# A message pass over 200,000 edges: two subtractions move from VectorE to GpSimd between its gathers, the additions of products vary by step, and one transpose in four becomes a copy

## The chip, the cores and the metric

The kernel runs on one core of a Trainium2 chip. The metric is the device time of the whole program in microseconds, as the median of several runs. The engines are named as in the profile: PE (TensorE; PEld is its weight load), DVE (VectorE), ACT (ScalarE), POOL (GpSimd), and SP, which issues DMAs.

## The reference, cut to what matters

The program is a graph network of four layers over 12,500 nodes and 200,000 edges, each layer followed by a residual addition and a layer norm. The change is in the third layer alone:

```python
xs = concat([x[src, :8], x[dst, :8]])                       # 16 scalars an edge
xv = concat([x[src, 8:].reshape(E, 8, 3), x[dst, 8:].reshape(E, 8, 3)])
h = 2.0 ** 0.5 * relu(emb @ W1 / 10.0 ** 0.5)               # 16 hidden units an edge
w = (h @ W2 / 16.0 ** 0.5).reshape(E, 7, 16, 8)             # seven 16x8 matrices an edge
s_out = PW_S * (einsum('eu,euw->ew', xs, wa_s) + INV_SQRT3 * einsum('eui,ei,euw->ew', xv, y1, wb_s))
...                                                          # g_out and v_out in the same manner
edge_ftr = concat([TANH_GAIN * tanh(s_out), (TANH_GAIN * tanh(g_out))[:, :, None] * v_out]) * norm[:, None]
out = segment_sum(edge_ftr, dst, N)
```

The weights of an edge depend on the edge through its 16 hidden units h. So the sum is over the units: what PE computes per unit from the edge's node values is multiplied by h and added over the 16 units.

## The kernel before, in words

The third layer's edge work is the function `l2_pass` (L1759). The edges lie in 128 partitions, 1,568 tiles of 128 edges. They are worked through in 28 chunks of 56 tiles; a chunk is 14 steps q of 4 tiles, and a step is two pairs, so that a chunk has 28 pairs `pr`. Every engine has its own program, written out by hand for one chunk and looped over two chunks (buffers b = 0 and 1); the order on each engine is the order in that code, and semaphores tie the engines together.

In step q of chunk c the engines do this:

- PE (`one_chunk` at L2001) makes the products of the first pair of step q + 1, the transposes of step q + 2, half of the sums of step q - 1, the products of the second pair, and the other half of the sums. `products` (L1973) writes two tiles of PSUM per pair. `transposes` (L1964) turns per tile the node values `zs` (two transposes of 64 columns, beside each other in the array) and the hidden units `hs` (one of 64 columns at L1969 and one more of the first 32 of them at L1970, which lands in rows 64 to 95). `sums` (L1989) adds the products over the units with an identity matrix: one float32 matmul of 192 columns for each unit that is left, `KEPT` = 12 of 16.
- DVE (`one_chunk` at L2324) multiplies the products of a pair with h and with the vector values (`pair`, L2257: L2267 and L2270), and after each second pair adds the last `ADDED` = 4 of the 16 units onto the first 4 (`add_units`, L2276). Between pairs it has the work of the next chunk, whose place is a pair number: two scans that fill in the destination rows (`fill_scan`, pairs 4 and 5), the terms and sums of the edge's direction (`p_terms`, `p_sum`, pairs 7 to 11; the last sends `p_done`), `unit_rest` (pairs 13 and 18), and `leave` (pair 19). Of the chunk before it has the six steps of `message`, pairs 12 to 17.
- ACT (`one_chunk` at L2140) copies the transposed tiles from PSUM to SBUF (`turn`: L2053 and L2054), takes the sums out (`summed`, L2058), and at half steps j = 2q + half does copies for the next chunk and the chunk before.
- POOL gathers the source rows of each tile by an indirect DMA (`row_gather`, L204, called at L1960), 56 a chunk into `z[b]`. It may begin chunk c + 3 when ACT has taken chunk c + 1 out of that buffer, which is at j = 4 of chunk c.

The split of the hidden units: h is kept as three bfloat16 parts, high, middle and low, in `hs`. ACT casts the high part (`unit_part` step 0, j = 10, sends `h_high`). `unit_rest` step 0 subtracts it from h into `rest_h` (L2283, sends `h_left`); ACT casts the middle part (`unit_part` step 1, j = 15, sends `h_mid`); `unit_rest` step 1 subtracts that too (L2286, sends `h_least`); ACT casts the low part (`unit_part` step 2, j = 20). `rest_h` lies in the tile `spread`, where the direction terms lay before, so step 0 waits for `p_done` as well. The chunk's first transposes come at step 12 of the chunk before.

There are three buffers of products in PSUM and three in SBUF (`prod`). DVE's pair of a step waits until PE has summed the step that used its buffer; in the last step of an odd chunk that is the step two back, elsewhere three or four, or two at a chunk's second step (L1859 and L1862).

Of the kernel before, what the change touches and what calls it, by code (L numbers as in the profile page):

```python
# [20 lines left out]
BF16 = mybir.dt.bfloat16  # L21
# [3 lines left out]
ALU = mybir.AluOpType  # L25
# [3 lines left out]
P = 128  # L29
# [35 lines left out]
def gnn_kernel(nc, x, src, dst, emb_t, attr3, attr5, edge_w, edge_w1, l0_w, lam, cheb_w, cheb_b,  # L65
# [25 lines left out]
    with top:  # L91
# [1667 lines left out]
        def l2_pass():  # L1759
# [6 lines left out]
            n = T // CH // 2  # L1766
            NC = 2 * n
            COLS = NG * M
            ADDED = 4
            KEPT = 16 - ADDED  # L1770
            gathered = gather_signals("l2")
            with ExitStack() as st:
                def sb(name, shape, dt=F32):
# [26 lines left out]

                p_t = ps("p_t", [P, 7 * 512])
                p_z = ps("p_z", [P, 1024], F16)
                p_zt, p_ht = p_z[:, 0:4 * P], p_z[0:96, 4 * P:8 * P].bitcast(BF16)
                p_sum6 = p_t[:, 6 * 512:6 * 512 + 4 * COLS]

                def scalar_part(k, t):
# [16 lines left out]
                h_left = signal("h_left")  # L1823
                h_mid = signal("h_mid")
                h_least = signal("h_least")
                units_added = signal("units_added")
                starts_in = signal("starts_in")
                starts_taken = signal("starts_taken")
# [42 lines left out]
                with nc.Block() as block:  # L1871
# [80 lines left out]
                    @block.gpsimd  # L1952
                    def _(pool):
                        row_gather(pool, fill[:], table, first_row[:]).then_inc(s_agg, 16)
                        with pool.Fori(0, n) as i:
                            for b in range(2):
                                pool.wait_ge(idx_in[b], 16 * (i + 1))
                                pool.sem_inc(chunks_begun, 1)
                                for t in range(CH):
                                    row_gather(pool, z[b][:, t, :], table, idx[b][:, t:t + 1]).then_inc(gathered[b], 16)  # L1960

                    @block.tensor
                    def _(pe):
                        def transposes(b, q):  # L1964

                            for t in range(4):
                                for half in range(2):
                                    nc.tensor.transpose(p_zt[64 * half:64 * half + 64, t * P:(t + 1) * P], zs[b][:, 4 * q + t, :], ident_h[:])
                                nc.tensor.transpose(p_ht[0:64, t * P:(t + 1) * P], hs[b][:, 4 * q + t, :], ident_b[:])  # L1969
                                last = nc.tensor.transpose(p_ht[64:96, t * P:(t + 1) * P], hs[b][:, 4 * q + t, 0:32], ident_b[:])  # L1970
                            last.then_inc(transposed, 1)

                        def products(c, b, q, half, first=False):  # L1973
# [15 lines left out]
                        def sums(c, b, q, part, first=False):  # L1989

                            if part == 0:
                                pe.wait_ge(units_added, c * Q + q + 1)
                                if q >= 1 or not first:
                                    pe.wait_ge(red_out, c * Q + q)
                            for k in range(part * KEPT // 4, (part + 1) * KEPT // 4):
                                last = nc.tensor.matmul(p_sum6, ident[:], prod[prod_buffer(b, q)][:, :, k, :],  # L1996
                                                        start=(k == 0), stop=(k == KEPT - 1))
                            if part == 3:
                                last.then_inc(red_made, 1)

# [44 lines left out]
                    def _(act):  # L2045
                        A = nc.scalar

                        def turn(c, q, first=False):

                            act.wait_ge(transposed, c * Q + q + 1)  # L2050
                            if q >= 2 or not first:
                                act.wait_ge(t_made, c * PRS + 2 * q - 2)
                            A.activation(zt[q % 2], p_zt, ACT.Copy)  # L2053
                            A.activation(ht[q % 2], p_ht, ACT.Copy).then_inc(zt_ready, 1)  # L2054

                        def summed(c, b, q):
                            act.wait_ge(red_made, c * Q + q + 1)
# [82 lines left out]
                        def one_chunk(c, b, times, first=False, second=False, more=True):  # L2140
                            before = not first
                            nxt, other = c + 1, 1 - b
                            for q in range(Q):
                                for half in range(2):
                                    j = 2 * q + half
                                    if half == 0:
                                        if q >= 2:
                                            summed(c, b, q - 2)
                                        elif before:
                                            summed(c - 1, other, Q - 2 + q)  # L2150
                                    elif q + 2 < Q:
                                        turn(c, q + 2, first)
                                    elif more:
                                        turn(nxt, q + 2 - Q)
                                    if more:
                                        if j in (0, 1):
                                            fill_mask_half(nxt, j, first or second)
                                        if j in (2, 3):
                                            starts_half(nxt, j - 2)
                                        if j == 4:  # L2160
                                            take(nxt, other, times, first)
                                        if j in (6, 7):
                                            dst_half(nxt, other, j - 6)
                                        if j == 10:
                                            unit_part(nxt, other, times, 0)
                                        if j == 13:
                                            high(nxt, other)
                                        if j == 15:
                                            unit_part(nxt, other, times, 1)
                                        if j == 20:  # L2170
                                            unit_part(nxt, other, times, 2)
                                        if j == 21:
                                            low(nxt, other)
                                    if before:
                                        if j == 5:
                                            tanhs(c - 1, other)
                                        if j in (8, 9):
                                            msg_mask_half(c - 1, j - 8)
                                        if j in (18, 19):
                                            msg_half(c - 1, j - 18, second)  # L2180

                        for half in range(2):
                            fill_mask_half(0, half, first=True)
# [28 lines left out]
                    def _(v):  # L2212
# [59 lines left out]
                        def add_units(c, b, q):  # L2272

                            v.wait_ge(t_used, c * PRS + 2 * q + 2)
                            of = prod[prod_buffer(b, q)]
                            V.tensor_tensor(of[:, :, 0:ADDED, :], of[:, :, 0:ADDED, :], of[:, :, KEPT:16, :], ALU.add).then_inc(units_added, 1)  # L2276

                        def unit_rest(c, b, step):

                            if step == 0:  # L2280
                                v.wait_ge(p_done, c + 1)
                                v.wait_ge(h_high, c + 1)
                                V.tensor_tensor(rest_h, hid[b][:], hs[b][:, :, 0:16], ALU.subtract).then_inc(h_left, 1)  # L2283
                            else:
                                v.wait_ge(h_mid, c + 1)
                                V.tensor_tensor(rest_h, rest_h, hs[b][:, :, 16:32], ALU.subtract).then_inc(h_least, 1)  # L2286

                        def message(c, b, times, step, first=False):

# [34 lines left out]
                        def one_chunk(c, b, times, first=False, second=False, more=True):  # L2324
# [4 lines left out]
                            for pr in range(PRS):  # L2329
# [1 line left out]
                                if pr % 2 == 1:  # L2331
                                    add_units(c, b, pr // 2)
                                if more:
                                    if pr in (4, 5):
                                        fill_scan(nxt, pr - 4)
                                    if pr == 7:
                                        p_terms(nxt, other, 0, times)
                                    if pr == 9:
                                        p_terms(nxt, other, 1, times)
                                    if pr in (10, 11):  # L2340
                                        p_sum(nxt, pr - 10)
                                    if pr == 13:
                                        unit_rest(nxt, other, 0)
                                    if pr == 18:
                                        unit_rest(nxt, other, 1)
                                    if pr == 19:
                                        leave(nxt, other)
                                if not first and 12 <= pr < 18:
                                    message(c - 1, other, here - other, pr - 12, second)

                        V.memset(mask[:, :, 0], 0.0)
                        V.memset(tail[:], 0.0).then_inc(fill_done, 1)
# [5 lines left out]
                            p_terms(0, 0, e, 0)  # L2358
                        for step in range(2):
                            p_sum(0, step)  # L2360
                        for step in range(2):
                            unit_rest(0, 0, step)
                        leave(0, 0)
                        one_chunk(0, 0, 0, first=True)
                        one_chunk(1, 1, 1, second=True)
# [80 lines left out]
```

## Time and profile before

| | us |
|---|---|
| median of 3 runs (range) | 13048.11 (13040.12 to 13057.17) |
| the profiled execution | 13047.31 |
| its span in the profile | 13045.3 |
| busy in the span: PE / DVE / ACT / POOL | 5831.6 / 5177.0 / 1973.6 / 7561.5 |
| the pass of the change, first to last take of a chunk (L2099) | 9484.7 to 12124.1 |

The page's busy shares are means over stages with different limits: in the message pass PE and DVE are busy, in the first quarter of the program POOL and the DMAs are, in the dense passes PE and the DMAs. Only the stretch from about 9485 us to 12340 us belongs to the change. The chain that ended last is that of the last layer and says nothing about this pass.

### The profile page before, as it was taken

What the parts mean: (1) busy time and instruction counts of PE and PEld (TensorE: products, weight loads), DVE (VectorE), ACT (ScalarE), POOL (GpSimd) and SP (SyncE); (2) the same over time, 40 slices, a digit from 0 to 9 for tenths busy, and PEclk for the clock granted to TensorE, in tenths of its full rate; (3) what the DMA queues carried; (4) which work ended last, traced back from release to release, by engine and by line L of the source; (5) the groups of instructions that cost most, each with busy time, mean ns of one, the idle gap of its engine ahead of it and who ended that gap; (6) DMA issues with size and microseconds to landing.
All of it is one profiled execution on the core that took longest, in us unless ns stands there. A gap on an engine that the chain in (4) does not pass through costs nothing. (4 is left out here: it accounts for less than half of the span.)

```text
span 13045.3 us, 195324 instructions
## 1 busy us (share of the span) xinstructions
PE 5831.6 (45%) x83238; PEld 5160.6 (40%) x83238; DVE 5177.0 (40%) x5503; ACT 1973.6 (15%) x2675; POOL 7561.5 (58%) x7346
## 2 busy tenths in 40 slices
PE   1000000310000199989994000000079999999779
PEld 0000000200000199989993000000057777777578
DVE  4455544930000211111101333232268888888611
ACT  1111111000000000000000112121034444444200
POOL 5777777677777621111213777777777666665140
PEclk6555555555555599989995555555589999999889
DMA  4555554000000299979993111111111111111179
GB/s 167 178 167 167 181 182 139 7 0 0 0 0 0 72 358 354 364 270 363 356 362 80 37 43 42 37 42 33 30 25 41 36 34 34 41 34 33 37 287 341
DMA packets 506705, 1622.48 MB, mean 124 GB/s; under 512 B 223736, under 2 KB 306032, under 8 KB 414768
## 3 DMA queue, kind: packets, MB, share of 16 engines
q1 hardware_dynamic: 252928, 1371.92, 28.2%
q0 software_dynamic: 234368, 154.18, 6.7%
q10 hardware_dynamic: 18608, 84.35, 1.7%
q8 instruction: 667, 10.93, 0.3%
q14 instruction: 134, 1.10, 0.0%
HBM read 1262.49 MB, written 352.41 MB: 124 GB/s over the span
## 5 line engine op out<-in xcount | busy, mean ns | idle before, releaser
L204 POOL DMA_INDIRECT z_l<-table,idx_l x1568 | 1812.2, 1156 | 791.1 <-issue 493.4
L204 POOL DMA_INDIRECT g_l<-table_l,idx_l x1568 | 1649.1, 1052 | 511.3 <-issue 501.2
L889 POOL DMA_INDIRECT adj<-worth,sq x1568 | 1546.1, 986 | 545.7 <-issue 509.6
L204 POOL DMA_INDIRECT g_gat<-table,idx_gat x1568 | 1479.5, 944 | 514.0 <-issue 499.8
L1996 PE MATMUL p_t<-prod,ident 128*128 128x192 f32 x9408 | 1740.4, 335 | 1.7 <-ACT sq L2058 1.7
L1996 PEld LDWEIGHTS p_t<-prod,ident 128*128 128x128 f32 x9408 | 1530.5, 192 | 55.6 <-issue 1.5
L1090 PE MATMUL p_h<-wd,emb_s 80*128 80x128 f32 x392 | 104.2, 444 | 2009.1 <-ACT hid L1146 1844.3
L1660 PE MATMUL pr<-diag,ones 128*128 128x256 f32 x2 | 1.2, 714 | 2110.5 <-DVE diag L1678 2110.5
L1090 PEld LDWEIGHTS p_h<-wd,emb_s 80*128 80x128 f32 x392 | 87.8, 327 | 2025.4 <-ACT hid L1146 1852.6
L2267 DVE TENSOR_TENSOR prod<-p_t,h_l 128x768 f32<-128x768 f32 x784 | 745.5, 951 | 328.3 <-PE p_t L1986 211.3
L414 PE MATMUL pc_l<-spread,cross_lo 128*128 128x448 f32 x28 | 25.3, 1023 | 1842.9 <-DVE spread L418 1678.6
L1660 PEld LDWEIGHTS pr<-diag,ones 128*128 128x128 f32 x2 | 0.5, 310 | 2110.8 <-DVE diag L1678 2110.8
L2270 DVE TENSOR_TENSOR prod<-p_t,xv 128x768 f32<-128x768 f32 x784 | 743.8, 949 | 0.0
L414 PEld LDWEIGHTS pc_l<-spread,cross_lo 128*128 128x128 f32 x28 | 7.4, 315 | 1858.7 <-DVE spread L418 1679.2
L1301 DVE MEMSET wc_mix<- 128x128 f32 x3 | 0.4, 165 | 1645.8 <-PEq L833 1645.8
L601 PE MATMUL acc_cheb0a<-parts_cheb0a,cells_cheb 128*128 128x96 bf16 x12348 | 541.9, 207 | 76.2 <-DVE parts_cheb0a L647 45.7
L601 PE MATMUL acc_l<-parts_l,cells_l 128*128 128x96 bf16 x12348 | 539.1, 207 | 76.5 <-DVE parts_l L647 44.9
L601 PEld LDWEIGHTS acc_cheb0a<-parts_cheb0a,cells_cheb 128*128 128x128 fp8e3 x12348 | 536.2, 99 | 86.0 <-issue 80.3
L601 PEld LDWEIGHTS acc_l<-parts_l,cells_l 128*128 128x128 fp8e3 x12348 | 531.6, 98 | 88.1 <-issue 85.1
L601 PE MATMUL acc_cheb0b<-parts_cheb0b,cells_cheb 128*128 128x96 bf16 x12348 | 537.0, 206 | 43.3 <-issue 28.7
L601 PE MATMUL acc_cheb1b<-parts_cheb1b,cells_cheb 128*128 128x96 bf16 x12348 | 536.4, 206 | 36.6 <-issue 25.3
L601 PE MATMUL acc_cheb1a<-parts_cheb1a,cells_cheb 128*128 128x96 bf16 x12348 | 535.8, 206 | 36.3 <-issue 27.6
(471 smaller groups left out, 12076.4 us busy)
## 6 DMA issues: line engine op xcount, KB each, us to landing
cells_cheb<-adj SPq DMA_DIRECT2D x560, 1344.0 KB
adj<-zeros SPq DMA_DIRECT2D x28, 7056.0 KB, 25.9
cells_l<-adj SPq DMA_DIRECT2D x140, 1344.0 KB
cells_cheb<-adj SPq DMA_DIRECT2D x56, 672.0 KB
gat_rows<-prod_gat ACTq DMA_DIRECT2D x28, 952.0 KB, 3.7
g_l<-table_l,idx_l POOLq DMA_INDIRECT x1568
start_rows<-zeros SPq DMA_DIRECT2D x28, 896.0 KB, 4.3
scanned_rows<-msg_l ACTq DMA_DIRECT2D x28, 896.0 KB, 9.7
```

What stands on the lines that cost most here:

```text
L204: return pool.indirect_dma_start(out=dest, out_offset=None, in_=table_ap, in_offset=bass.IndirectOffsetOnAxis(ap=index, axis=0))
L414: nc.tensor.matmul(banks[k % 2][:, 0:JB * n], cross_lo[:], spread[:, k * JB * n:(k + 1) * JB * n], start=True, stop=True).then_inc(s_pe, 1)
L601: last = nc.tensor.matmul(acc[r % 2][:, c // HELD, h * 3 * D:(h + 1) * 3 * D], cells[n % SLOTS][:, (i * m + c) * P:(i * m + c + 1) * P], m ...
L889: pool.indirect_dma_start(out=adj, out_offset=bass.IndirectOffsetOnAxis(ap=cell[:, t:t + 1], axis=0), in_=worth_u[:, t:t + 1], in_offset=N ...
L1090: last = nc.tensor.matmul(p_h[:, g * P:(g + 1) * P], emb_s[b][:, (g0 + g) * P:(g0 + g + 1) * P], wd[:], start=True, stop=True)
L1301: nc.vector.memset(w[:], 0.0)
L1660: nc.tensor.matmul(pr[:].rearrange("p a q -> p (a q)"), ones[:], diag[:].rearrange("p a q -> p (a q)"), start=True, stop=True).then_inc(s_ ...
L1996: last = nc.tensor.matmul(p_sum6, ident[:], prod[prod_buffer(b, q)][:, :, k, :], start=(k == 0), stop=(k == KEPT - 1))
L2267: V.tensor_tensor(into[:, :, :, 0:24], scalar_pair(k).rearrange("p t (k f) -> p t k f", k=16), h_b, ALU.mult)
L2270: V.tensor_tensor(into.rearrange("p t u (i w) -> p (t u) i w", w=M)[:, :, 3:6, :], w_uw, x_ui, ALU.mult).then_inc(t_used, 1)
```

## The change

1. The number of units that DVE adds before PE sums varies by step, from 2 to 7 instead of 4 in each; PE sums the 16 - ADDED[q] that are left.
2. The two subtractions of `unit_rest` are made by POOL. It makes them before the gathers t = 28 and t = 42 of chunk c for the units of chunk c - 1, with the same waits as DVE had. Those of chunk 0 come between the gathers of chunk 0 and of chunk 1, those of the last chunk after all gathers.
3. The transpose at L1970 goes. ACT writes the rows 64 to 95 of `ht` with a third copy, from rows 0 to 31 of the transposed units.
4. Places in the order change: on DVE `fill_scan` is at pairs 4 and 6, `p_terms` at 8 and 10, `p_sum` at 11 and 12, `leave` at 16, `message` at 14, 15, 18, 19, 20 and 22; ACT's parts move by one or two half steps, `low` from 21 to 18, `msg_half` from 18 and 19 to 23 and 24.

```diff
-            ADDED = 4
-            KEPT = 16 - ADDED
+            STEPS = (14, 15, 18, 19, 20, 22)
+            ADDED = (7, 7, 3, 3, 4, 2, 3, 2, 2, 2, 3, 3, 7, 7)
...
-                p_zt, p_ht = p_z[:, 0:4 * P], p_z[0:96, 4 * P:8 * P].bitcast(BF16)
+                p_zt, p_ht = p_z[:, 0:4 * P], p_z[0:64, 4 * P:8 * P].bitcast(BF16)
...
-                        with pool.Fori(0, n) as i:
+                        def unit_rest(c, b, step):
+
+                            if step == 0:
+                                pool.wait_ge(p_done, c + 1)
+                                pool.wait_ge(h_high, c + 1)
+                                pool.sem_inc(rests_begun, 1)
+                                nc.gpsimd.tensor_tensor(rest_h, hid[b][:], hs[b][:, :, 0:16], ALU.subtract).then_inc(h_left, 1)
+                            else:
+                                pool.wait_ge(h_mid, c + 1)
+                                pool.sem_inc(rests_begun, 1)
+                                nc.gpsimd.tensor_tensor(rest_h, rest_h, hs[b][:, :, 16:32], ALU.subtract).then_inc(h_least, 1)
+
+                        def one_chunk(c, b, times, before=True):
+                            pool.wait_ge(idx_in[b], 16 * (times + 1))
+                            pool.sem_inc(chunks_begun, 1)
+                            for t in range(CH):
+                                if before and t in (28, 42):
+                                    unit_rest(c - 1, 1 - b, (t - 28) // 14)
+                                row_gather(pool, z[b][:, t, :], table, idx[b][:, t:t + 1]).then_inc(gathered[b], 16)
+                        one_chunk(0, 0, 0, before=False)
+                        for step in range(2):
+                            unit_rest(0, 0, step)
+                        one_chunk(1, 1, 0, before=False)
+                        with pool.Fori(1, n) as i:
                             for b in range(2):
-                                pool.wait_ge(idx_in[b], 16 * (i + 1))
-                                pool.sem_inc(chunks_begun, 1)
-                                for t in range(CH):
-                                    row_gather(pool, z[b][:, t, :], table, idx[b][:, t:t + 1]).then_inc(gathered[b], 16)
+                                one_chunk(2 * i + b, b, i)
+                        for step in range(2):
+                            unit_rest(NC - 1, 1, step)
...
-                                nc.tensor.transpose(p_ht[0:64, t * P:(t + 1) * P], hs[b][:, 4 * q + t, :], ident_b[:])
-                                last = nc.tensor.transpose(p_ht[64:96, t * P:(t + 1) * P], hs[b][:, 4 * q + t, 0:32], ident_b[:])
+                                last = nc.tensor.transpose(p_ht[:, t * P:(t + 1) * P], hs[b][:, 4 * q + t, :], ident_b[:])
...
-                            for k in range(part * KEPT // 4, (part + 1) * KEPT // 4):
+                            kept = 16 - ADDED[q]
+                            for k in range(part * kept // 4, (part + 1) * kept // 4):
...
-                            A.activation(ht[q % 2], p_ht, ACT.Copy).then_inc(zt_ready, 1)
+                            A.activation(ht[q % 2][0:64], p_ht, ACT.Copy)
+                            A.activation(ht[q % 2][64:96], p_ht[0:32], ACT.Copy).then_inc(zt_ready, 1)
...
-                            V.tensor_tensor(of[:, :, 0:ADDED, :], of[:, :, 0:ADDED, :], of[:, :, KEPT:16, :], ALU.add).then_inc(units_added, 1)
+                            some = ADDED[q]
+                            V.tensor_tensor(of[:, :, 0:some, :], of[:, :, 0:some, :], of[:, :, 16 - some:16, :], ALU.add).then_inc(units_added, 1)
...
-                                    if pr == 13:
-                                        unit_rest(nxt, other, 0)
-                                    if pr == 18:
-                                        unit_rest(nxt, other, 1)
-                                    if pr == 19:
+                                    if pr == 16:
                                         leave(nxt, other)
-                                if not first and 12 <= pr < 18:
-                                    message(c - 1, other, here - other, pr - 12, second)
+                                if not first and pr in STEPS:
+                                    message(c - 1, other, here - other, STEPS.index(pr), second)
```

## Rows read from the trace of the kernel before

**Rows 1.** Busy time by stretch: length, PE, PEld, DVE, ACT, POOL, clock, DMA share, GB/s.

```profile
10000.00:11000.00 1000.00, 955.35 (x6796) 774.36 (x6794) 871.00 (x912) 447.67 (x637) 675.63 (x578) 0.98 0.16 38
```

**Rows 2.** The take of a chunk (L2099), all 28 of them: durations, first and last start; its waits.

```profile
L2099 ACT ACTIVATE zsf<-z_l x28: 575/592/601, 9484.7 to 12124.1; 128x448 f32<-128x448 f32 x28
...
  DMA z_l<-table,idx_l: 107.3, 2
```

**Rows 3.** Timeline of ACT, the take in chunk 6: start us, duration us, what, count.

```profile
10144.31 0.60 ACT L2099 ACTIVATE zsf<-z_l 128x448 f32<-128x448 f32 x1
```

**Rows 4.** Timeline of PE over one step, 10503 to 10512 us.

```profile
10502.95 2.17 PE L1996 MATMUL p_t<-prod,ident 128*128 128x192 f32 x12
10504.96 0.33 PE L1985 MATMUL p_t<-w_terms,spread 128*128 128x384 f16 x1
...
10505.50 0.25 PE L1968 MATMUL p_z<-ident_h,zs 128*64 128x128 f16 x2
10505.58 0.22 PE L1969 MATMUL p_z<-ident_b,hs 128*64 128x128 bf16 x1
10505.73 0.23 PE L1970 MATMUL p_z<-ident_b,hs 128*32 128x128 bf16 x1
...
10507.05 2.22 PE L1996 MATMUL p_t<-prod,ident 128*128 128x192 f32 x12
...
10511.56 0.33 PE L1985 MATMUL p_t<-w_terms,spread 128*128 128x384 f16 x1
```

**Rows 5.** Timeline around the end of PE's loop over two chunks, 10028 to 10042 us.

```profile
10028.21 0.53 ACT L2058 ACTIVATE agg<-p_t 128x192 f32<-128x192 f32 x1 [3.52 <-PE p_t L1996]
...
10031.92 0.37 PE L1985 MATMUL p_t<-w_terms,spread 128*128 128x384 f16 x1 [3.75 <-issue]
...
10035.04 4.10 PE L1996 MATMUL p_t<-prod,ident 128*128 128x192 f32 x12
...
10041.62 0.54 ACT L2058 ACTIVATE agg<-p_t 128x192 f32<-128x192 f32 x1 [4.41 <-PE p_t L1996]
```

**Rows 6.** Waits between 9600 and 12300 us: waiting line, its releaser, us, times, longest.

```profile
DVE prod L2267 <- PE p_t L1996: 113.7, 27, 5.9
PEld p_t L1985 <- DVE prod L2270: 91.7, 104, 2.3
```

**Rows 7.** DVE's groups between 9400 and 12400 us: busy us, mean ns, idle before.

```profile
L2276 DVE TENSOR_TENSOR prod<-prod 128x768 f32<-128x768 f32 x392 | 375.6, 958 | 13.4
...
L2224 DVE SCALAR_TENSOR_TENSOR zf<-fill,same,zf 128x32 f32<-128x32 f32 x28 | 7.8, 278 | 38.8 <-issue 30.5 <-ACT zf L2090 8.3
```

**Rows 8.** Timeline of DVE ahead of the first chunk, 9493 to 9500 us.

```profile
9493.97 1.09 DVE L2283 TENSOR_TENSOR spread<-h_l,hs 128x896 f32<-128x896 f32 x1
9496.54 1.09 DVE L2286 TENSOR_TENSOR spread<-spread,hs 128x896 f32<-128x896 f32 x1 [1.47 <-ACT hs L2135]
9497.55 2.08 DVE L2255 TENSOR_TENSOR zsf<-zsf,zs 128x1792 f32<-128x1792 f32 x1
```

**Rows 9.** POOL's gathers of this pass, from the page's costliest groups.

```profile
L204 POOL DMA_INDIRECT z_l<-table,idx_l x1568 | 1812.2, 1156 | 791.1 <-issue 493.4 <-DMA idx_l<-src_rows 297.7
```

**Rows 10.** Timeline of POOL and DVE, 10503 to 10506 us.

```profile
10503.08 0.94 POOL L204 DMA_INDIRECT z_l<-table,idx_l  x1 [0.30 <-issue]
...
10504.20 0.96 DVE L2276 TENSOR_TENSOR prod<-prod 128x768 f32<-128x768 f32 x1
10504.33 1.66 POOL L204 DMA_INDIRECT z_l<-table,idx_l  x1 [0.30 <-issue]
```

**Rows 11.** POOL's instructions that are no DMA, whole span, by group.

```profile
L876 POOL MEMSET zeros<- 128x1792 f32 x1 | 1.6, 1587 | 0.0
...
L262 POOL MEMSET ones<- 128x128 f32 x1 | 0.2, 195 | 0.0
...
L272 POOL TENSOR_SCALAR_AFFINE_SELECT ident<-ones 128x128 f32<-128x128 f32 x1 | 0.3, 292 | 0.1
```

**Rows 12.** ACT's copy of the transposed units (L2054), 9000 to 12500 us, by group.

```profile
L2054 ACT ACTIVATE agg<-p_z 96x512 bf16<-96x512 bf16 x392 | 228.8, 584 | 0.0
```

More of the change, by code:

```diff
@@ L1825, in l2_pass @@
                 h_least = signal("h_least")
+                rests_begun = signal("rests_begun")
                 units_added = signal("units_added")
@@ L1994, in sums @@
                                     pe.wait_ge(red_out, c * Q + q)
-                            for k in range(part * KEPT // 4, (part + 1) * KEPT // 4):
+                            kept = 16 - ADDED[q]
+                            for k in range(part * kept // 4, (part + 1) * kept // 4):
                                 last = nc.tensor.matmul(p_sum6, ident[:], prod[prod_buffer(b, q)][:, :, k, :],
-                                                        start=(k == 0), stop=(k == KEPT - 1))
+                                                        start=(k == 0), stop=(k == kept - 1))
                             if part == 3:
@@ L2161, in one_chunk @@
                                             take(nxt, other, times, first)
-                                        if j in (6, 7):
-                                            dst_half(nxt, other, j - 6)
-                                        if j == 10:
+                                        if j in (8, 9):
+                                            dst_half(nxt, other, j - 8)
+                                        if j == 12:
                                             unit_part(nxt, other, times, 0)
-                                        if j == 13:
+                                        if j == 14:
                                             high(nxt, other)
-                                        if j == 15:
+                                        if j == 16:
                                             unit_part(nxt, other, times, 1)
+                                        if j == 18:
+                                            low(nxt, other)
                                         if j == 20:
                                             unit_part(nxt, other, times, 2)
-                                        if j == 21:
-                                            low(nxt, other)
                                     if before:
@@ L2176, in one_chunk @@
                                             tanhs(c - 1, other)
[L2177 to L2180, printed above, removed]
+                                        if j in (10, 11):
+                                            msg_mask_half(c - 1, j - 10)
+                                        if j in (23, 24):
+                                            msg_half(c - 1, j - 23, second)
                         for half in range(2):
@@ L2275, in add_units @@
                             of = prod[prod_buffer(b, q)]
-                            V.tensor_tensor(of[:, :, 0:ADDED, :], of[:, :, 0:ADDED, :], of[:, :, KEPT:16, :], ALU.add).then_inc(units_added, 1)
[L2278 to L2286, printed above, removed]
+                            some = ADDED[q]
+                            V.tensor_tensor(of[:, :, 0:some, :], of[:, :, 0:some, :], of[:, :, 16 - some:16, :], ALU.add).then_inc(units_added, 1)
                         def message(c, b, times, step, first=False):
@@ L2333, in one_chunk @@
                                 if more:
[L2334 to L2341, printed above, removed]
-                                    if pr == 13:
-                                        unit_rest(nxt, other, 0)
-                                    if pr == 18:
-                                        unit_rest(nxt, other, 1)
-                                    if pr == 19:
+                                    if pr in (4, 6):
+                                        fill_scan(nxt, (pr - 4) // 2)
+                                    if pr in (8, 10):
+                                        p_terms(nxt, other, (pr - 8) // 2, times)
+                                    if pr in (11, 12):
+                                        p_sum(nxt, pr - 11)
+                                    if pr == 16:
                                         leave(nxt, other)
-                                if not first and 12 <= pr < 18:
-                                    message(c - 1, other, here - other, pr - 12, second)
+                                if not first and pr in STEPS:
+                                    message(c - 1, other, here - other, STEPS.index(pr), second)
                         V.memset(mask[:, :, 0], 0.0)
@@ L2360, in _ @@
                             p_sum(0, step)
-                        for step in range(2):
-                            unit_rest(0, 0, step)
                         leave(0, 0)
```

## The prediction

> **What bounds the kernel now.** I read the busy time by stretch first, then the timeline of one step, then the waits, then POOL. Ten chunks in the middle of the pass have PE busy 95.5%, DVE 87.1%, POOL 67.6% and ACT 44.8%, at a granted clock of 0.98 [rows 1]. A chunk takes (12124.1 - 10144.3) / 20 = 99.0 us, by the takes of chunk 7 and of chunk 27 [rows 2, 3]. In an undisturbed step PE goes from one first product to the next in 10511.56 - 10504.96 = 6.60 us, without a gap [rows 4], so 14 steps are 92.4 us. Once in two chunks, at the end of PE's loop, PE stands for 3.75 us with nothing to wait for ("issue"), and then runs a half step of sums in 4.10 us that takes 2.17 elsewhere, the lower of its two clock levels (1.2 for 2.4 GHz); the two takes-out of sums are 13.41 us apart there instead of 6.60 [rows 5]. That is 6.8 us, 3.4 a chunk. 92.4 + 3.4 = 95.8. The last 3.2 us are PE's waits for DVE, 91.7 us over 27 chunks [rows 6]. So PE is the bound, DVE touches it in places, and both count.
>
> **PE.** Six units of sums take 10504.96 - 10502.95 = 2.01 us, 0.335 a unit [rows 4]. ADDED adds up to 55 instead of 56, so PE sums 169 units a chunk instead of 168: +0.3 us. The four tiles of transposes take 10507.05 - 10505.50 = 1.55 us, 0.39 each: 0.08 from the pair of L1968 to L1969, 0.15 to L1970, 0.15 to the next tile [rows 4]. A transpose of the same size follows its neighbour by 0.08 where it has the same 64 columns; only in front of and behind the one of 32 columns are there 0.15. I take it that both gaps are the change of width, so that without L1970 a tile takes 0.14 and 0.25 goes; the lower end is that only its own 0.15 goes. 56 tiles: 14.0 us, at least 8.4. PE then needs 92.4 + 0.3 - 14.0 + 3.4 = 82.1 us a chunk (87.7 at the lower end).
>
> The Trainium skill's page "TensorEngine Tiling (Array Packing)", Key Properties, says that a change of tiling mode, not just of tile, drains TensorE. By that rule both gaps go, by the lower end one; the two 0.15 us around the one narrow transpose agree with it.
>
> **DVE.** 0.871 of 99.0 is 86.2 us busy a chunk [rows 1]. The two subtractions go, 1.01 us each from start to next start [rows 8]: -2.0. A unit more or less in an addition is (2.08 - 0.96) / 1024 elements x 192 = 0.21 us, by the addition of 768 and the subtraction of 1792 elements [rows 7, 8]; one unit fewer in all is -0.2. The additions of 7 (some 1.5 us) lie in steps 0, 1, 12 and 13, where DVE has nothing else, those of 2 (0.5 us) where it has scans and messages. This and the moves of the side work cost nothing in themselves; they even out DVE's steps, which is where today's 3.2 us of waits come from. 84.0 us are left. Outside the busy time stands a stop of 30.5 / 13 = 2.3 us once in two chunks (L2224, "issue") [rows 7]: +1.2.
>
> New on DVE is that POOL reads SBUF for longer. The trace shows the reverse case: a gather that begins within L2276, which has two SBUF inputs, takes 1.66 us instead of 0.94, until that is over, while beside L2267 and L2270 (one input from PSUM) it takes 0.94 [rows 10]. So I expect DVE's two-input instructions to wait for a subtraction on POOL that began first. Bounds: 0, and both subtractions in full, 4.4 us. After `p_done` DVE first has a pair of 1.7 us, so step 0 costs little; step 1 comes at any place. I take 1.5.
>
> The Trainium skill's page "SBUF — State Buffer", Who interferes with whom, states this for both directions: whichever starts first holds the shared read interface for its whole instruction. This speaks against the change: by it a part of the 2.0 us taken from DVE comes back as waiting.
>
> PE's loop end also reaches DVE. DVE has up to three pairs of products ahead, 3 x 1.73 us, so of the 6.8 us I let 3 through, 1.5 a chunk. At the last step of an odd chunk DVE waits for the sums two steps back (part of the 113.7 us of [rows 6]); with PE done sooner 0.3 is left. DVE: 84.0 + 1.2 + 1.5 + 1.5 + 0.3 = 88.5 us a chunk.
>
> **POOL.** 56 gathers at 1.156 and 0.315 us of issue (493.4 / 1568) are 82.4 us [rows 9]; today it waits 10 to 16 us a chunk for an index list. A subtraction of 896 elements isn't in the trace. A fill costs (1587 - 195) / 1664 = 0.84 ns an element and 0.09 us fixed, one input and one output (292 - 90) / 128 = 1.6 ns [rows 11]; a third stream at the same step gives 2.4 ns, 2.2 us. Bounds: 0.8 (a fill) and 5 (twice the estimate, for a strided bfloat16 operand and for waiting on DVE). I take 2.2 and 0.3 of issue: 87.4 us a chunk.
>
> The Trainium skill's "GPSIMD Engine Reference", Performance versus the Vector engine, has 4497 ns for an addition of 2048 float32 elements; scaled, an estimate of 2.0 us and the same sum within 0.4.
>
> **What is queued behind POOL's new waits.** Behind the wait for `p_done` at t = 28 stand 28 gathers, which ACT takes only about three steps after they are done; nobody else waits. The second subtraction is more pressing. From `p_done` (half way through step 6) it ends after 2.2 + 14 x 1.47 + 2.2 = 25 us; ACT wants it at j = 20, 3.5 steps or 22 us on. ACT then stands in front of `turn` for 3 us. That is about its slack there: the transposed tiles are wanted a step later, and cast and copies take 3 us. So the wait costs nothing as long as POOL is in time for `p_done`, and beyond that each us of POOL's lateness comes out one for one: POOL's 87.4 is a bound of its own.
>
> **ACT.** The third copy reads 512 elements as L2054 does, 0.58 us [rows 12], 14 a chunk: 8 us more on an engine that is busy 44 of 99. It is in the chain from transposes to products, which has a step of time and needs 0.6 + 2 x 0.58. Nothing, at most 0.58 a step where side work stands before it.
>
> **The sum.** PE 82.1, POOL 87.4, DVE 88.5. With three engines so close I add 0.4 for handing over: 88.9 us a chunk, 10.1 less. 26 such chunks: -263. The last chunk has no next one beside it and PE paces it: 10 steps and more at 1.0, -10. At the start POOL makes the subtractions of chunk 0 before it gathers chunk 1, and the pass waits for that gather already (107.3 us in two waits [rows 2]): `p_done` comes at about 9494 us [rows 8], 9 us behind the end of the first gathers, then 2.2, a cast, 2.2: +15. POOL then enters chunk 2 late, reaches t = 28 after `p_done` and makes chunk 0 wait: about +9. Together -249 us. The profiled execution took 13047.3 us, its span and 2.0 around it, 0.8 less than the median: 12,800.
>
> **Rivals.**
>
> - A: only the narrow transpose's own 0.15 us goes. PE needs 87.7 and its waits for DVE stay at 3.2: 90.9 a chunk. 26 x 8.1 + 8 - 24 = 195 less: 12,852. For it: LDWEIGHTS or data type might make the gap. Against: L1968 to L1969 also changes the type, and takes 0.08 [rows 4].
> - B: POOL sets the pace with subtractions of 5 us: 82.4 + 10.6 = 93.0 a chunk, 26 x 6.0 + 10 - 24 = 142 less: 12,905. For it: POOL's gathers are held up by DVE already (1.156 mean for 0.94), and no row bounds two inputs from above.
> - C, slower: going from a gather to arithmetic and back costs POOL a fixed time, a drain of descriptor work or code to be brought in, since the two never alternate in the trace. It decides from 8.0 us a subtraction (82.4 + 16.0 = 98.4, with the 24 of the start); at 12 us a chunk takes 106.4 and the kernel 13,253. Against: nothing stands between a fill and an affine select (0.1 us and less idle [rows 11]), but no gather stands between those either. The Trainium skill's "GPSIMD Engine Reference", Instruction dispatch, gives some 6 us for the first call into newly loaded code; paid at every change both ways it would make 14 us a subtraction and 13,350. No run here shows it for a gather.
> - D: it doesn't do what it says: the second subtraction reaches ACT so late in every chunk that PE waits what it had gained; then about the time of before.
>
> **How the numbers follow.** Forecast 0.58, A 0.18, B 0.14, C 0.07, D 0.03. 0.2%, 26 us, is what can be told from no change here. Faster 0.58 + 0.18 + 0.14 = 0.90, same 0.03, slower 0.07. The range goes from 12,700 (85 us a chunk: no blocking, DVE's own 84.0 and a little) to 12,950 (just above B); C, D and the tail of B stay out.
>
> **What would show it.** Right: a step of PE without its waits of (6.60 - 1.0) us at 12 units; four tiles of transposes in 0.55 to 0.65 us instead of 1.55; PE's share of waits for DVE up, its busy share down to some 88%; subtractions on POOL of 2 to 3 us; a chunk of 88 to 90; first take of chunk 1 some 15 us later. Wrong: tiles still of 0.23 us and more (A), subtractions over 4 us or idle time around them (B, C), PE waiting for ACT at step 11 (D), DVE instructions of several us beside POOL's (the blocking was sized too low), or DVE's busy share under 93% with nobody else at the bound.

## The result, and the profile after

The changed kernel takes 12,897.9 us (median of 4, 12,882.1 to 12,906.1) where the kernel before takes 13,045.5 beside it: a ratio of 0.9884 [0.9867, 0.9901], 148 us less. The sum had given 249 less.

A chunk now takes (11979.2 - 10124.2) / 20 = 92.75 us instead of 99.0; 88.9 was predicted. The take of chunks and the busy time by stretch (PE, PEld, DVE, ACT, POOL), which answer to [rows 1 to 3]:

```profile
L2123 ACT ACTIVATE zsf<-z_l x28: 575/588/602, 9476.9 to 11979.2; 128x448 f32<-128x448 f32 x28
...
10124.21 0.58 ACT L2123 ACTIVATE zsf<-z_l 128x448 f32<-128x448 f32 x1
...
10000.00:12000.00 2000.00, 1808.65 (x13342) 1561.14 (x13343) 1866.01 (x1897) 1119.82 (x1668) 1552.76 (x1231) 0.96 0.15 39
```

PE's busy share fell from 95.5 to 90.4%, DVE's rose to 93.3%. Neither is full. PE's timeline in a free step, which answers to [rows 4]:

```profile
10329.40 0.33 PE L2007 MATMUL p_t<-w_terms,spread 128*128 128x384 f16 x1
...
10329.94 0.25 PE L1991 MATMUL p_z<-ident_h,zs 128*64 128x128 f16 x2
10330.02 0.22 PE L1992 MATMUL p_z<-ident_b,hs 128*64 128x128 bf16 x1
...
10330.13 0.22 PE L1992 MATMUL p_z<-ident_b,hs 128*64 128x128 bf16 x1
...
10330.50 2.22 PE L2019 MATMUL p_t<-prod,ident 128*128 128x192 f32 x12
...
10335.01 0.33 PE L2007 MATMUL p_t<-w_terms,spread 128*128 128x384 f16 x1
```

The transposed tiles follow at 0.11 us, four take 10330.50 - 10329.94 = 0.56 instead of 1.55, and from the first product of the step (10329.40) to that of the next are 5.61 us. PE got all that was forecast. POOL's part of the middle of the pass, first before, then after (busy us, mean ns, idle before):

```profile
L204 POOL DMA_INDIRECT z_l<-table,idx_l x1145 | 1345.4, 1175 | 656.7 <-issue 360.3 <-DMA idx_l<-src_rows 296.5
```

```profile
L204 POOL DMA_INDIRECT z_l<-table,idx_l x1189 | 1473.7, 1239 | 384.5 <-issue 383.2
L1962 POOL TENSOR_TENSOR spread<-h_l,hs 128x896 f32<-128x896 f32 x21 | 39.8, 1894 | 29.0 <-DVE zsf L2274 28.9
L1966 POOL TENSOR_TENSOR spread<-spread,hs 128x896 f32<-128x896 f32 x21 | 39.7, 1892 | 0.4
```

The wait for an index list (296.5) is gone. A gather takes 1.239 us, with 0.322 of issue in front of it, and 56 x (1.239 + 0.322) + 2 x 1.89 = 91.2 us. With 28.9 / 21 = 1.4 of waiting for `p_done` these are 92.6 of the 92.75, so POOL has next to no time left over. What that does to the others, at step 10 of an even chunk:

```profile
10364.27 2.36 POOL L204 DMA_INDIRECT z_l<-table,idx_l  x1 [0.30 <-issue]
10366.94 0.94 POOL L204 DMA_INDIRECT z_l<-table,idx_l  x1 [0.30 <-issue]
10367.90 1.89 POOL L1966 TENSOR_TENSOR spread<-spread,hs 128x896 f32<-128x896 f32 x1
10369.82 0.95 ACT L2162 ACTIVATE hs<-spread 128x896 bf16<-128x896 f32 x1 [8.11 <-POOL spread L1966]
...
10372.46 0.50 PE L2007 MATMUL p_t<-w_terms,spread 128*128 128x384 f16 x1 [5.07 <-ACT agg L2078]
```

The lines are to be followed downwards. POOL ends its subtraction at 10369.79. ACT, which had waited 8.11 us for it, casts, then copies the transposed tiles (L2076 to L2078). PE, which had waited 5.07 us for them, goes on, and it goes on slowly: from 10,372 to 10,376 us its granted clock is 0.50, the lower of its two levels (1.2 for 2.4 GHz). L2007 takes 0.50 us there instead of 0.33, and the half step of 12 matmuls behind it 4.21 instead of 2.22. And DVE, first beside the same subtraction, then beside that of the next chunk:

```profile
10367.62 2.79 DVE L2301 TENSOR_TENSOR prod<-prod 128x576 f32<-128x576 f32 x1
...
10458.68 2.42 DVE L2331 SCALAR_TENSOR_TENSOR zf<-tail,same,zf 128x32 f32<-128x32 f32 x1
10459.11 1.90 POOL L1966 TENSOR_TENSOR spread<-spread,hs 128x896 f32<-128x896 f32 x1
```

An addition that takes 0.76 us without a subtraction beside it (e5 below) takes 2.79, and an instruction of 32 columns 2.42 instead of 0.27.

### The profile page after: what moved, and what is told of

Read it like the earlier page. It is cut to its first block and busy times, and to the rows that moved or that the text cites. A ratio compares the mean times of both kernels' runs of the same rounds, so it can differ in the third digit from the quotient of the medians.

```text
span 12880.3 us, 192743 instructions
## 1 busy us (share of the span) xinstructions
PE 5522.6 (43%) x81726; PEld 5032.5 (39%) x81726; DVE 5185.9 (40%) x5447; ACT 2183.3 (17%) x3067; POOL 7765.6 (60%) x7402
## 5 line engine op out<-in xcount | busy, mean ns | idle before, releaser
L204 POOL DMA_INDIRECT z_l<-table,idx_l x1568 | 1911.3, 1219 | 505.9 <-issue 503.4
L2019 PE MATMUL p_t<-prod,ident 128*128 128x192 f32 x9464 | 1790.3, 341 | 14.7 <-ACT sq L2082 6.9
L2019 PEld LDWEIGHTS p_t<-prod,ident 128*128 128x128 f32 x9464 | 1578.0, 196 | 82.5 <-issue 18.0
L2291 DVE TENSOR_TENSOR prod<-p_t,h_l 128x768 f32<-128x768 f32 x784 | 744.6, 950 | 195.8 <-PE p_t L2008 162.1
L2294 DVE TENSOR_TENSOR prod<-p_t,xv 128x768 f32<-128x768 f32 x784 | 742.9, 948 | 0.0
L2007 PE MATMUL p_t<-w_terms,spread 128*128 128x384 f16 x1568 | 446.8, 337 | 282.9 <-ACT agg L2078 123.3
```

What stands on the lines that cost most here:

```text
L204: return pool.indirect_dma_start(out=dest, out_offset=None, in_=table_ap, in_offset=bass.IndirectOffsetOnAxis(ap=index, axis=0))
L2007: nc.tensor.matmul(scalar_part(k, t), zt[q % 2][:, tile * P:(tile + 1) * P], w_terms[:], start=True, stop=True)
L2291: V.tensor_tensor(into[:, :, :, 0:24], scalar_pair(k).rearrange("p t (k f) -> p t k f", k=16), h_b, ALU.mult)
L2294: V.tensor_tensor(into.rearrange("p t u (i w) -> p (t u) i w", w=M)[:, :, 3:6, :], w_uw, x_ui, ALU.mult).then_inc(t_used, 1)
```

## The experiments

Each median stands against the kernel before on the same chip. The kernel before takes 13,048.3 us beside e1 to e4, 13,054.2 beside e5 to e8 and 13,058.8 beside e9 to e11, so medians of different groups can be off against each other by some 10 us. Chunk is the time from take to take over the last 20 chunks of each trace.

| run | chunk us | median us | ratio [95%] |
|---|---|---|---|
| changed kernel | 92.75 | 12,897.9 | 0.9884 [0.9867, 0.9901] |
| e1 second subtraction at gather 36 | 91.8 | 12,863.4 | 0.9860 [0.9844, 0.9877] |
| e2 subtractions on DVE | 88.8 | 12,765.0 | 0.9789 [0.9772, 0.9805] |
| e3 before + transposes | 93.0 | 12,864.6 | 0.9865 [0.9849, 0.9882] |
| e4 before + subtractions on POOL | 98.7 | 13,051.5 | 1.0003 [0.9994, 1.0013] |
| e5 fills in place of subtractions | 91.2 | 12,841.6 | 0.9838 [0.9821, 0.9854] |
| e6 subtractions at 20 and 28 | 91.5 | 12,839.7 | 0.9839 [0.9822, 0.9855] |
| e7 e2 with 48 units added | 89.3 | 12,773.9 | 0.9785 [0.9769, 0.9801] |
| e8 e2 with the old transposes | 97.3 | 13,001.2 | 0.9961 [0.9947, 0.9975] |
| e9 e2 with 50 gathers | 87.9 | 12,742.3 | 0.9760 [0.9743, 0.9776] |
| e10 changed, 50 gathers | 90.1 | 12,831.6 | 0.9823 [0.9807, 0.9840] |
| e11 e10 with 28 and 36 | 88.5 | 12,781.1 | 0.9790 [0.9774, 0.9806] |

**e1.**

```diff
-                                if before and t in (28, 42):
-                                    unit_rest(c - 1, 1 - b, (t - 28) // 14)
+                                if before and t in (28, 36):
+                                    unit_rest(c - 1, 1 - b, (t - 28) // 8)
```

> The changed kernel with POOL's second subtraction before gather 36 instead of 42. In the changed kernel the second subtraction ends some 26 us after the first began, and in each of the 26 regular chunks ACT's cast at j = 20 begins 0.03 us behind it: ACT waits for POOL, 5.9 us a chunk, and PE then waits for the turned tiles. Theory L (the late second subtraction is what costs): it now ends 14 us after the first, ACT no longer waits, a chunk falls from 92.6 to 88.5 to 89.5 us, and the kernel takes 12,785 to 12,815 us. Rival P (POOL's own pace, 56 gathers of 1.54 us and two subtractions, 90.5 us): a chunk takes 90.5 at least, 12,845. Rival S (DVE blocked beside POOL's subtractions, 2.6 us a chunk): the place changes nothing, 92 to 93 us a chunk, 12,880 to 12,910.

The chunk fell by 0.95 us, where theory L gave 3 to 4. P holds: POOL's own 56 x (1.257 + 0.314) + 3.8 = 91.8 us is the whole chunk. The lateness moved to the first subtraction. ACT now waits for it in 25 chunks, and less for the second, where in the changed kernel it waits for the second nearly alone (159.4 us in 27 waits, 6.5 in 2 for the first):

```profile
ACT hs L2159 <- POOL spread L1962: 168.5, 25, 8.7
...
ACT hs L2162 <- POOL spread L1966: 80.2, 25, 4.2
```

**e2.**

```diff
+                                    if pr in (13, 17):
+                                        unit_rest(nxt, other, (pr - 13) // 4)
...
-                        def one_chunk(c, b, times, before=True):
+                        with pool.Fori(0, n) as i:
+                            for b in range(2):      # 56 gathers, nothing between them
```

> The changed kernel with both subtractions back on DVE, at pairs 13 and 17. Theory L: DVE has 2.0 us more of work and 2.6 us less of blocking, ACT's cast at j = 20 waits for nobody, POOL's gathers are ahead again and the start is 17 us shorter: 88.5 to 90 us a chunk, 12,770 to 12,820. Rival S agrees on the sign but, if blocking alone is it, gives 92 us a chunk and with the start 12,870. Rival 'the move itself is the gain': slower than the changed kernel, 94 us and more a chunk, 12,920 and above.

3.9 us a chunk and 133 us faster than the changed kernel: the move to POOL cost nearly as much as the whole change brought. It is the fastest version with the full computation, and faster than both kernels. POOL is at its bound even so: 56 x (1.275 + 0.31) = 88.8 us, and ACT waits for gathers at its take, 63.9 us in 17 chunks. 88.8 is also the forecast's chunk of 88.9, reached without the move.

**e3.** The kernel before with the diff's PE and ACT lines for the transposes.

> The kernel before with the transpose of 32 columns replaced by ACT's third copy, nothing else. PE's free step falls from 6.60 to 5.6 us, so PE needs 82 us a chunk; DVE with its two subtractions needs 86.2 and 1.2 of its stop. Theory (the transpose carries the whole gain, DVE is the next bound): 90.5 to 92.5 us a chunk instead of 99.0, 12,825 to 12,880 us. Rival (DVE's uneven steps with 4 units each give half of it back, so the varied additions are needed): 94 to 96 us, 12,920 to 12,970.

12,864.6: this one part alone is worth 184 us, more than all parts together with POOL's. Its chunk of 93.0 lies between the two expectations, its median within the theory's. PE waits 267.4 us for DVE in 264 places, so DVE is what holds it.

**e4.** The kernel before with POOL's `unit_rest` and its places, and none of DVE's.

> The kernel before with the two subtractions on POOL before gathers 28 and 42, nothing else moved. PE bounds it with 6.60 us a step, so ACT reaches j = 20 later and the second subtraction is in time. Theory: DVE is 2 us lighter and 2 to 3 us blocked, a chunk takes 98 to 99.5 us as before, the start costs 15 to 18 us more: 13,040 to 13,075. Rival (DVE's relief removes part of the 3.2 us that PE waits for DVE): 96.5 to 97.5 us a chunk, 12,990 to 13,025.

No difference, as expected: PE is the bound (96.6% busy), POOL has time over and waits for `p_done` (303.0 us in 25 waits). The price of the move shows only once PE is faster.

**e5.**

```diff
-  nc.gpsimd.tensor_tensor(rest_h, hid[b][:], hs[b][:, :, 0:16], ALU.subtract).then_inc(h_left, 1)
+  nc.gpsimd.memset(spread[:, 0:2080], 0.0).then_inc(h_left, 1)
```

and the same for the second.

> The changed kernel where POOL writes zeros over 2080 columns of the same tile in place of each subtraction, about as long (0.09 + 2080 x 0.84 ns = 1.84 us for 1.9) but reading no SBUF; the middle and low parts of the hidden units are thereby left out. Theory S (DVE's two-input instructions are held by POOL's reads): L2331, L2314 and the additions of 3 units fall back to 0.27, 1.55 and 0.76 us, DVE's busy time by 2.6 us a chunk; a chunk of 90.5 to 91.5 us, since POOL's own 91 us remain, 12,830 to 12,860. Rival: POOL holds DVE by its writes as well, durations and time as in the changed kernel, 92.7 a chunk, 12,890.

DVE's instructions in the changed kernel and then in e5 (busy us, mean ns):

```profile
L2301 DVE TENSOR_TENSOR prod<-prod 128x576 f32<-128x576 f32 x108 | 104.9, 971 | 3.7
...
L2331 DVE SCALAR_TENSOR_TENSOR zf<-tail,same,zf 128x32 f32<-128x32 f32 x21 | 31.5, 1498 | 0.0
```

```profile
L2301 DVE TENSOR_TENSOR prod<-prod 128x576 f32<-128x576 f32 x110 | 83.4, 758 | 3.8
...
L2331 DVE SCALAR_TENSOR_TENSOR zf<-tail,same,zf 128x32 f32<-128x32 f32 x22 | 5.9, 270 | 0.0
...
L1966 POOL MEMSET spread<- 128x2080 f32 x23 | 42.6, 1851 | 7.4 <-ACT hs L2159 7.4
```

A fill as long as the subtraction holds nothing up. So it is the subtraction that holds DVE's instructions, by something that a fill doesn't do. That it is the reading of SBUF is what sets the two apart; an instruction on POOL with one input was not tried. DVE's busy time falls from 0.933 x 92.75 = 86.5 to 0.919 x 91.2 = 83.8 us a chunk: the blocking is 2.7, for the 2.0 that the move had taken off. The chunk gains 1.5, as expected. POOL's gathers became shorter too, 1.214 us instead of 1.239, and 56 of them make 1.4 of the 1.5.

**e6.** As e1, with gathers 20 and 28.

> The changed kernel with POOL's subtractions before gathers 20 and 28 instead of 28 and 42. With 28 and 36 a chunk took 91.8 us, ACT still waited 6.7 us a chunk for the first subtraction and 3.2 for the second, and POOL was busy or issuing all the time. Theory P (POOL's pace: 56 gathers of 1.25 + 0.3 us and 3.8 us of subtractions, 91 us): a chunk stays at 91 to 91.8 us, ACT no longer waits for POOL's subtractions but POOL's gathers come late to the take; 12,840 to 12,870. Rival L (lateness of the subtractions is what costs): 89 to 90 us a chunk, 12,790 to 12,815.

P again, on its number: 56 x (1.255 + 0.307) + 3.9 = 91.4 of 91.5 us. ACT waits for none of the subtractions, but 85.1 us for gathers.

**e7.**

```diff
-            ADDED = (7, 7, 3, 3, 4, 2, 3, 2, 2, 2, 3, 3, 7, 7)
+            ADDED = (6, 6, 3, 2, 3, 2, 2, 2, 1, 2, 3, 2, 7, 7)
```

> The kernel of e2 (subtractions on DVE) with 48 instead of 55 units added on DVE: (6,6,3,2,3,2,2,2,1,2,3,2,7,7). A chunk of e2 took 88.8 us with DVE busy 96.3% and POOL's gathers at 1.275 + 0.3 us, 88 us a chunk, ACT waiting for gathers at its take. Theory (POOL, slowed by DVE's two-input work, and DVE share the bound): DVE 1.5 us lighter, gathers 1 us a chunk shorter, PE 2.3 us heavier but below the bound: 87.3 to 88.3 us a chunk, 12,725 to 12,755. Rival (PE with its loop end is as near): 88.8 to 90 us, 12,765 to 12,800.

89.3 us, the rival's number and no different from e2. The theory had gathers become shorter with a lighter DVE. DVE is busy 94.3% instead of 96.3, but the gathers still take 1.279 us, and 56 x (1.279 + 0.313) = 89.2 us is again the whole chunk. Whether PE is as near a bound, as the rival says, isn't shown by this.

**e8.** e2 with the kernel before's lines for the transposes.

> The kernel of e2 with the transpose of 32 columns back on PE (and ACT's third copy gone): the varied additions and moved places alone, against the kernel before. Theory: PE's free step is 6.6 us at 12 units, PE needs 92.7 + 3 us; the evened steps of DVE take away the 3.2 us of waits: 95.5 to 97 us a chunk, 12,960 to 12,995 us. Rival: additions of 2 units in the busy steps make PE's own steps uneven and nothing is gained, 98 to 99.5 us, 13,030 to 13,060.

97.3 us and 13,001 lie between, just above the theory's range: the varied additions and places are worth 1.7 us a chunk while PE is the bound, and 93.0 - 88.8 = 4.2 (e3 against e2) once the narrow transposes have gone.

**e9 to e11.** Fewer gathers, from the third chunk on:

```diff
-                            for t in range(CH):
+                            for t in range(FEW if before else CH):      # FEW = 50
...
-                            act.wait_ge(gathered[b], 16 * CH * (times + 1))
+                            act.wait_ge(gathered[b], 16 * CH + 16 * FEW * times)
```

> The kernel of e2 (subtractions on DVE) with only 50 of 56 rows gathered from the third chunk on; the other six tiles of z keep old rows. Theory P (POOL, with gathers slowed to 1.275 + 0.3 us, sets e2's 88.8 us a chunk; ACT waits for gathers at its take): 6 x 1.58 = 9.5 us fewer on POOL, DVE becomes the bound at 85.6 busy and 1.2 of its stop: 86.8 to 88 us a chunk, 12,700 to 12,740. Rival (DVE and PE's loop end are the bound, POOL's waits are incidental): 88.5 to 89 us, 12,755 to 12,775.

> The changed kernel with 50 of 56 rows gathered from the third chunk on, the subtractions still before gathers 28 and 42. POOL has 82 us of work a chunk instead of 91.3, but its second subtraction still ends 26 us after the first began. Theory P alone: 88.5 to 89.5 us a chunk, 12,790 to 12,820. Theory L (both: PE waits for the late second subtraction even when POOL has time): 90.5 to 92.5 us, 12,840 to 12,890, ACT still waiting some 4 to 8 us a chunk at L2162.

> As e10, and the second subtraction before gather 36. POOL is early and the subtraction in time, so neither POOL's pace nor lateness is left, only DVE's blocking (2.6 us for 2.0 of relief). Theory: like e9 within 1 us: 87.5 to 89 us a chunk, and 15 to 18 us more at the start, 12,745 to 12,790. Rival (blocked DVE instructions stall more than their own length): 90 us and more, 12,820.

e9's chunk is 0.9 us below e2's, its median 2 us above the theory's range. POOL's pace costs e2 little, and DVE, 96.8% busy, is the bound right behind as far as its busy share tells. The intervals of e9 and e2 overlap; the chunks of the two traces tell them apart. e10, with 9.4 us taken off POOL, falls from 92.75 to 90.1, between its two expectations and nearer L's. ACT still waits for the late second subtraction:

```profile
ACT hs L2163 <- POOL spread L1967: 113.7, 26, 8.8
```

In e11 that wait is gone and a chunk takes 88.5 us, within its theory. This is e1's theory L's number, but only where POOL has time.

## Why the prediction was right in sign and 100 us too low

The path from 92.75 to e9's 87.9 gives the parts: 2.6 us POOL's pace (changed kernel to e10), 1.6 the late second subtraction (e10 to e11), 0.6 that the subtractions are on POOL at all (e11 to e9: 2.7 of blocking for 2.0 of relief). How the first two share depends on the order. With the subtraction moved first they are 0.95 (e1) and then 3.3 (e1 to e11), so only their sum, 4.2, is firm.

- **PE: right.** 0.56 us for four tiles (0.55 to 0.65 forecast), 5.61 a step. Rival A fell: both gaps around the narrow transpose went, (1.55 - 0.56) / 4 = 0.25 us a tile.
- **DVE: right within 1 us.** Its busy time was taken as 84.0 and 1.5 of blocking; it is 86.5. Blocking is 2.7, by e5, within the bounds of 0 to 4.4. The reverse of the case in [rows 10], inferred there, is now shown, and so is that it takes two SBUF inputs on DVE: the 38 instructions of L2291 and L2294, with one input from PSUM, that overlap a subtraction behind 10,000 us take 0.95 us as elsewhere, while 22 additions take 1.81 and 12 of L2331 take 2.42. What failed is the conclusion that DVE sets the chunk.
- **POOL's subtraction: right.** 1.89 us against 2.2. Rival C fell: going from gathers to arithmetic costs nothing, 0.02 us lie between a gather's end and the subtraction and 0.16 between it and the next gather. Rival B's cause fell too, but its numbers came almost exactly, POOL setting the pace at 93.0 us a chunk and 12,905 us. It was the gathers and the wait behind them, not subtractions of 5 us. The range had been drawn up to just above B, so that the time lies in it is in part luck.
- **POOL's gathers: this step failed.** "56 gathers at 1.156 and 0.315 us of issue are 82.4 us" took over the mean of the kernel before. It is 56 x (1.239 + 0.322) = 87.4 us: 5.0 more, and 91.2 with the subtractions instead of 87.4. Some 1.1 of the 5.0 could have been read beforehand. The mean over the pass contains the gathers of the first two chunks, which run before DVE is at work (1.014 between 9,400 and 9,550 us), and between 10,000 and 12,000 us it is 1.175 already. Another 0.4 is issue, and the rest is a longer hold. A gather that begins beside no DVE instruction with two SBUF inputs takes 0.944 us in both kernels; one that begins within such an instruction ends 0.82 us behind it (median). These are 24 of 56 in a chunk before and 22 after. So not more gathers are held: each is held longer, 1.672 us instead of 1.483. The time added behind DVE's additions of products is 4.8 and 4.6 us a chunk, that behind DVE's other instructions 8.3 and 11.8. DVE's busy share alone does not explain it, as e3 shows:

```profile
L204 POOL DMA_INDIRECT z_l<-table,idx_l x1154 | 1373.4, 1190 | 488.2 <-issue 365.9 <-DMA idx_l<-src_rows 122.3
```

  e3 has the old additions and places. Its DVE is busy 92.4%, but its gathers take 1.190, and 8.1 us a chunk are added behind DVE's other instructions. e8 has the new additions and places and the old transposes: DVE is busy 87.9%, the gathers take 1.209, and 11.6 us are added there. e2, with both, has 12.1, and 1.275. Against the 1.175 of the kernel before, the transposes alone add 0.015 us to a gather, DVE's new order of work alone (parts 1 and 4 of the change) 0.034, and both together 0.100. The prediction's "This and the moves of the side work cost nothing in themselves" holds for DVE and not for POOL. Whether it is the lengths of the additions or the places of the side work is open; no run has one without the other, and e7, with 48 units added in the new places, leaves a gather at 1.279. That POOL's pace, and not DVE's 88.5, sets the chunk is what e1, e6 and e10 show.
- **The wait behind POOL: half right.** The end of the second subtraction was reckoned 25 us behind `p_done`, POOL being in time for it, and ACT's slack 3 us. In the trace it is 26.3 us in every second chunk, where POOL waits for `p_done` (10,248.92 to 10,275.24), and 31.0 in the chunks between, where POOL comes to its first subtraction 3.4 us late (`p_done` at 10,338.78, subtraction at 10,342.13, end of the second at 10,369.79). The slack was used up and PE waited too. The prediction had named this ("beyond that each us of POOL's lateness comes out one for one") and reckoned none of it. Its price is the 1.6 us of e10 to e11, in which POOL is in time. Nor had it reckoned that PE's clock falls behind such a wait: PE is busy 83.9 us a chunk in the changed kernel at a mean granted clock of 0.96, and 81.9 at 0.99 in e11. D's sign, PE waiting for ACT, came, but at 1.6 us a chunk and not at the whole gain.
- **The start** was reckoned at +24. The take of chunk 1 comes 91.5 us behind that of chunk 0 instead of 75.9, 15.6 later, as forecast. Chunk 7 is taken 647.3 us behind chunk 0 instead of 659.6; six regular chunks would have given -37, so the start costs some 25.
- **The sum by itself:** 26 x 3.85 = 100 us make up the difference between 249 and 148. The two profiled executions lie 165 us apart; in them the stretch behind the last take is 20 us shorter, where 10 was forecast.

## What to carry to other kernels

Before work is moved to an engine with "idle" time, ask what its present instructions will cost beside the new order of its neighbours, and don't take over a mean: here 56 gathers grew by 5 us a chunk, with as many of them held as before and each held longer. An engine's spare time is to be set against the new period, not today's: POOL had some 15 us to spare in 99, and none in the 88.8 of e2, the kernel without its new work. Changes that come together want to be tried apart: one of these three was worth 184 us, one 100 on top of it, and the third took 133 back.

## What the runs showed that I had not expected

- A DVE instruction with two SBUF inputs is held by a subtraction on POOL that begins after it by the record: L2301 begins at 10367.62, POOL's subtraction at 10367.90, and the addition takes 2.79 us. That an instruction starts first in the profile does not show that the other waits for it.
- The same two subtractions cost nothing (e4) or 3.9 us a chunk (the changed kernel against e2), by who bounds the kernel.
- PE's halt at its loop's end (3.62 us of "issue" in the changed kernel, 3.75 before) still comes through in good part: the takes-out of sums there lie 9.98 us apart where 4.63 is the free distance, 5.35 more, against 6.8 before. What it costs a chunk that POOL paces isn't shown.
